# The last chunk's output stage of an attention + FFN layer, split into two halves of 256 tokens

## The reference, cut to what matters

```python
h = _layernorm(x) * (1 + ca) + sa
x = x + ga * _L0_attn_ref(h, Wq, Wp, bp)        # 16 heads of 16, softmax over all 4096 tokens
h = _layernorm(x) * (1 + cb) + sb
x = x + gb * _L0_ffn_ref(h, ...)
# _L0_ffn_ref: residual + 0.5 * (silu(layernorm(h)*gamma+beta @ w1 + b1) @ w2 + b2), hidden width 1024
```

## Time and profile before

| | |
|---|---|
| time, median of 3 runs | 2159.39 us (2160.18, 2159.39, 2154.71) |
| time of the profiled execution | 2153.64 us |
| its span, first to last instruction | 2151.0 us |
| busy in the span | PE 91%, ACT 92%, DVE 18%, POOL 4% |
| mean granted TensorE clock | 0.986 of full speed |
| last two exponentials of the attention start | 2083.94 us |

### The profile page before, as it was taken

How to read it: one execution, slowest core, us unless ns; L and a number is a source line. 1 busy time by engine, 2 the same in 40 slices (tenths; PEclk the granted TensorE clock), 3 DMA queues, 4 the chain that set the end, 5 groups by cost and what they waited for, 6 DMA issues and landing times.

```text
span 2151.0 us, 32823 instructions
## 1 busy us (share of the span) xinstructions
PE 1965.8 (91%) x13703; PEld 537.4 (25%) x13703; DVE 392.8 (18%) x873; ACT 1979.6 (92%) x2161; POOL 91.7 (4%) x42
## 2 busy tenths in 40 slices
PE   5578889999999999999999999999999999999995
PEld 3411112222222222222222222222222222222233
DVE  7501000410022100411004100311004100221003
ACT  2489999999999999999999999999999999999971
POOL 2000000100000000100001000100001000010001
PEclk9889999999999999999999999999999999999998
DMA  3261111111211111212121121212121112111100
GB/s 129 80 180 48 48 40 48 44 43 40 53 46 47 49 49 44 51 32 58 39 55 43 44 53 39 49 46 51 40 57 41 47 39 54 44 39 39 29 11 10
DMA packets 121860, 107.38 MB, mean 50 GB/s; under 512 B 23025, under 2 KB 120945, under 8 KB 121457
## 3 DMA queue, kind: packets, MB, share of 16 engines
q1 hardware_dynamic: 121712, 105.29, 18.0%
HBM read 96.56 MB, written 8.65 MB: 49 GB/s over the span
## 4 chain that ended last, share of the span: by engine, by line
ACT 48%; PE 39%; issue 7%; DVE 1%; DMA 0%; SPq 0%; ACTq 0%
ACT attend_probs L686 47%; PE attend_sums L724 18%; PE attend_scores L712 10%; PE attend_out L756 5%; PE attend_out L751 2%; PE attend_out L742 1%; ACT attend_half_tanh L671 1%; PE attend_scores L751 1%; PE attend_scores L756 1%; PE attend_out L747 0%; PE attend_scores L742 0%; DVE attend_rsqrt_work L92 0%; DVE attend_st L874 0%; DVE attend_rs L87 0%; PE attend_scores L747 0%
## 5 line engine op out<-in xcount | busy, mean ns | idle before, releaser
L686 ACT ACTIVATE attend_probs<-attend_scores 128x1024 f32<-128x1024 f32 x2048 | 1909.1, 1046 | 39.7 <-PE attend_scores L712 23.6
L724 PE MATMUL attend_sums<-attend_probs,values 128*17 128x512 f32 x8192 | 1010.8, 597 | 0.0
L712 PE MATMUL attend_scores<-asks,keys 64*128 64x512 f16 x4096 | 658.2, 383 | 109.5 <-ACT attend_probs L686 69.2
L712 PEld LDWEIGHTS attend_scores<-asks,keys 64*128 64x128 f16 x4096 | 149.5, 94 | 883.3 <-ACT attend_probs L686 778.0
L724 PEld LDWEIGHTS attend_sums<-attend_probs,values 128*17 128x17 f32 x8192 | 171.7, 96 | 394.8 <-issue 390.4
L756 PE MATMUL attend_out<-w,hidden 128*128 128x256 f32 x448 | 125.9, 403 | 0.0
L751 PE MATMUL attend_out<-attend_ffn_in,w 128*128 128x512 f32 x224 | 124.6, 638 | 0.0
L846 DVE COPY attend_sums_sb<-attend_sums 128x512 f32<-128x512 f32 x32 | 22.1, 691 | 499.2 <-PE attend_sums L724 499.2
L910 DVE TENSOR_SCALAR attend_half_in<-attend_out,b_col 128x512 f32<-128x512 f32 x56 | 42.0, 750 | 351.1 <-PE attend_out L751 350.1
L756 PEld LDWEIGHTS attend_out<-w,hidden 128*128 128x128 f32 x448 | 75.9, 189 | 95.1 <-issue 89.3
L920 DVE TENSOR_TENSOR attend_base<-attend_out,attend_base 128x512 f32<-128x512 f32 x14 | 9.7, 691 | 393.2 <-PE attend_out L756 393.2
(11 more groups left out here) (129 smaller groups left out, 568.7 us busy)
## 6 DMA issues: line engine op xcount, KB each, us to landing
keys<-parts_dram SPq DMA_DIRECT2D x768, 64.0 KB
keys<-parts_dram SPq DMA_DIRECT2D x256, 56.0 KB
asks<-parts_dram SPq DMA_DIRECT2D x192, 64.0 KB
start_x_in<-L_attn_x SPq DMA_DIRECT2D x8, 512.0 KB, 6.5
parts_dram<-start_q_parts SPq DMA_DIRECT2D x16, 256.0 KB, 2.5
attend_x_now<-L_attn_x SPq DMA_DIRECT2D x8, 512.0 KB, 4.2
out<-attend_base SPq DMA_DIRECT2D x16, 256.0 KB, 2.7
asks<-parts_dram SPq DMA_DIRECT2D x64, 56.0 KB
```

The costliest lines, as they stand in the source:

```text
L686: act.activation(probs[n % P_RING], ps_scores[:, 2 * slot:2 * slot + 2, :], ACT.Exp, scale=scale)\
L712: last = pe.matmul(ps_scores[:, 2 * (n % S_RING) + b, :], keys[rows, part % K_RING, hq, col:col + P], asks[rows, group * Q_HEADS + hq, :], ...
L724: last = pe.matmul(ps_sums[32 * hq:32 * hq + E1, :], values[:, j + STEPS * b, (gg % Q_GROUPS) * Q_HEADS + hq, :], probs[n % P_RING][:, b, ...
```

## The change

The tail works on two halves of 256 tokens (two tiles each). DVE does the whole chain residual, norm, modulation, norm for half 0 and then for half 1. PE transposes, does up and down for half 0, then the same for half 1; the up matmuls have 256 columns instead of 512. The evacuation of the transposed `z2` goes from DVE to ACT (Identity with scale and bias, L697 of the changed kernel). SiLU has 256 columns, 16 instructions instead of 8. `base` of the last chunk is computed by DVE, per half, behind both norm chains; POOL does it for the other seven chunks as before. The second half's projection and down result are in `ps_out`. New semaphores order this. Code of the other chunks is unchanged.

```diff
@@ GpSimd
                     pool.tensor_tensor(x_now, x_now, wide(bp_ga[:, :]), ALU.add).then_inc(xb_ready, 1)
+                    if o == G - 1:
+                        break
@@ ScalarE
-                o = G - 1
-                for f in range(FT):
-                    act.wait_ge(up_mm, FT * o + f + 1)
-                    act.activation(hidden[:, f, :], ps_scores[:, f % 4, :], ACT.Silu, bias=b1_col[:, f:f + 1]).then_inc(tail_hidden, 1)
+                for half in range(2):
+                    cols = slice(half * D, (half + 1) * D)
+                    act.wait_ge(tail_turned, half + 1)
+                    for k in range(DC):
+                        act.activation(ffn_in[:, k, cols], ps_scores[:, 4, k * D:(k + 1) * D], ACT.Identity,
+                                       bias=beta_col[:, k:k + 1], scale=gamma_col[:, k:k + 1]).then_inc(tail_in, 1)
+                    for f in range(FT):
+                        act.wait_ge(tail_up, FT * half + f + 1)
+                        act.activation(hidden[:, f, cols], ps_scores[:, f % 4, 0:D], ACT.Silu, bias=b1_col[:, f:f + 1]).then_inc(tail_hidden, 1)
@@ TensorE
-                pe.wait_ge(z2_ready, o + 1)
-                for k in range(DC):
-                    turn_z2(k, ps_scores[:, 4 + k, :])
-                pe.wait_ge(fi_ready, 2 * o + 2)
...
+                for half in range(2):
+                    cols = slice(half * D, (half + 1) * D)
+                    pe.wait_ge(z2_ready, o + half + 1)
+                    wait(pe, tail_in, DC * half)
+                    for k in range(DC):
+                        for t in range(2):
+                            last = pe.transpose(ps_scores[:, 4, k * D + t * P:k * D + (t + 1) * P],
+                                                z2[:, 2 * half + t, k * P:(k + 1) * P], ident[:, :])
+                    last.then_inc(tail_turned, 1)
+                    pe.wait_ge(tail_in, DC * (half + 1))
                     for f in range(FT):
+                        wait(pe, tail_hidden, FT * half + f - 3)
+                        for k in range(DC):
+                            last = pe.matmul(ps_scores[:, f % 4, 0:D], w1[:, k, f * P:(f + 1) * P], ffn_in[:, k, cols],
+                                             start=(k == 0), stop=(k == DC - 1))
+                        last.then_inc(tail_up, 1)
+                    for t in range(2):
+                        for f in range(FT):
+                            if t == 0:
+                                pe.wait_ge(tail_hidden, FT * half + f + 1)
+                            last = pe.matmul([ps_scores[:, 5, :], ps_out][half][:, t * D:(t + 1) * D],
+                                             hidden[:, f, (2 * half + t) * P:(2 * half + t + 1) * P], w2[:, f, :],
+                                             start=(f == 0), stop=(f == FT - 1))
+                    last.then_inc(tail_down, 1)
@@ VectorE
+                for half in range(2):
+                    pair = slice(2 * half, 2 * half + 2)
+                    residual(o, half, [ps_scores[:, 2, :], ps_out][half])
+                    dve.wait_ge(x1_ready, 2 * o + half + 1)
+                    stats_of_half(x1, half, 0)
+                    scaled_half(z1, x1, half, 0).then_inc(z1_ready, 1)
...
+                    dve.tensor_tensor(hid[:, pair, :], z1[:, pair, :], wide2(mod[:, 4, :]), ALU.mult).then_inc(scaled, 1)
...
+                    dve.tensor_tensor(hid[:, pair, :], hid[:, pair, :], wide2(mod[:, 3, :]), ALU.add).then_inc(hid_ready, 1)
...
+                    stats_of_half(hid, half, 1)
+                    scaled_half(z2, hid, half, 1).then_inc(z2_ready, 1)
+                dve.wait_ge(y_stored, 32 * o)
+                for half in range(2):
...
+                    dve.tensor_tensor(base[:, pair, :], hid[:, pair, :], wide2(mod[:, 5, :]), ALU.mult).then_inc(tail_base, 1)
...
+                    dve.tensor_tensor(base[:, pair, :], base[:, pair, :], wide2(b2_gb[:, :]), ALU.add).then_inc(tail_base, 1)
...
+                    dve.tensor_tensor(base[:, pair, :], base[:, pair, :], x1[:, pair, :], ALU.add).then_inc(tail_base, 1)
...
+                    dve.wait_ge(tail_down, half + 1)
+                    dve.tensor_tensor(base[:, pair, :], [ps_scores[:, 5, :], ps_out][half].rearrange("p (t d) -> p t d", d=D),
+                                      base[:, pair, :], ALU.add).then_inc(y_ready, 1)
```

More of the change, by code:

```diff
@@ L584, in adaln_layer @@
          base_step, z2_ready, z2_turned, fi_ready, up_mm, half_ready, tanh_done, hidden_ready, down_mm, y_ready, y_stored,
-         tail_hidden) = (sem(n) for n in (
+         tail_turned, tail_in, tail_up, tail_hidden, tail_down, tail_base) = (sem(n) for n in (
              "xn_in", "xb_ready", "att_turned", "af_ready", "proj_mm", "x1_ready", "n_stats", "n_mom", "n_rstd", "z1_ready",
              "scaled", "hid_ready", "base_step", "z2_ready", "z2_turned", "fi_ready", "up_mm", "half_ready", "tanh_done",
-             "hidden_ready", "down_mm", "y_ready", "y_stored", "tail_hidden"))
+             "hidden_ready", "down_mm", "y_ready", "y_stored", "tail_turned", "tail_in", "tail_up", "tail_hidden", "tail_down", "tail_base"))
         z2 = z1
@@ L825, in _ @@
                         pe.wait_ge(af_ready, 2 * o + 2)
-                    project(t, ps_scores[:, 2 + t // 2, (t % 2) * D:(t % 2 + 1) * D])
-                pe.wait_ge(z2_ready, o + 1)
-                for k in range(DC):
-                    turn_z2(k, ps_scores[:, 4 + k, :])
-                pe.wait_ge(fi_ready, 2 * o + 2)
-                for f in range(FT):
-                    if f >= 4:
-                        pe.wait_ge(tail_hidden, f - 3)
-                    for k in range(DC):
-                        up(f, k, ps_scores[:, f % 4, :])
@@ L836, in _ @@
-                for t in range(GT):
-                    for f in range(FT):
-                        if t == 0:
-                            pe.wait_ge(tail_hidden, f + 1)
-                        down(t, f, ps_scores[:, 4 + t // 2, (t % 2) * D:(t % 2 + 1) * D])
+                    project(t, [ps_scores[:, 2, :], ps_out][t // 2][:, (t % 2) * D:(t % 2 + 1) * D])
+                for half in range(2):
+                    cols = slice(half * D, (half + 1) * D)
+                    pe.wait_ge(z2_ready, o + half + 1)
+                    wait(pe, tail_in, DC * half)
+                    for k in range(DC):
+                        for t in range(2):
[3 more added lines that the diff above has]
+                    pe.wait_ge(tail_in, DC * (half + 1))
+                    for f in range(FT):
+                        wait(pe, tail_hidden, FT * half + f - 3)
[11 more added lines that the diff above has]
+                    last.then_inc(tail_down, 1)
@@ L995, in _, with wide2 @@
                     take_att(o, k, ps_scores[:, k, :])
[L996 to L1003, removed]
+                def wide2(v):
+                    return v.unsqueeze(1).broadcast_to([P, 2, D])
@@ new lines, in stats_of_half @@
+                def stats_of_half(src, half, r):
+                    n = 2 * o + 2 * half + r
+                    tiles = range(2 * half, 2 * half + 2)
+                    for t in tiles:
+                        last = dve.bn_stats(st2[:, t, :], src[:, t, :])
+                    last.then_inc(n_stats, 1)
+                    dve.wait_ge(n_stats, n + 1)
+                    for t in tiles:
+                        last = dve.bn_aggr(mo2[:, r, t, :], st2[:, t, :])
+                    last.then_inc(n_mom, 1)
+                    dve.wait_ge(n_mom, n + 1)
+                    pair = slice(2 * half, 2 * half + 2)
+                    rsqrt(dve, rs2[:, r, pair], mo2[:, r, pair, 1], rsqrt_work2[:, :, pair], n_rstd, n)
@@ new lines, in scaled_half @@
+                def scaled_half(to, src, half, r):
+                    for t in range(2 * half, 2 * half + 2):
+                        last = dve.tensor_scalar(to[:, t, :], src[:, t, :], mo2[:, r, t, 0:1], rs2[:, r, t:t + 1], ALU.subtract, ALU.mult)
+                    return last
+                dve.wait_ge(z2_turned, 2 * o)
+                dve.wait_ge(base_step, 3 * o)
+                for half in range(2):
+                    pair = slice(2 * half, 2 * half + 2)
+                    residual(o, half, [ps_scores[:, 2, :], ps_out][half])
+                    dve.wait_ge(x1_ready, 2 * o + half + 1)
+                    stats_of_half(x1, half, 0)
+                    scaled_half(z1, x1, half, 0).then_inc(z1_ready, 1)
+                    dve.wait_ge(z1_ready, o + half + 1)
+                    dve.tensor_tensor(hid[:, pair, :], z1[:, pair, :], wide2(mod[:, 4, :]), ALU.mult).then_inc(scaled, 1)
+                    dve.wait_ge(scaled, o + half + 1)
+                    dve.tensor_tensor(hid[:, pair, :], hid[:, pair, :], wide2(mod[:, 3, :]), ALU.add).then_inc(hid_ready, 1)
+                    dve.wait_ge(hid_ready, o + half + 1)
+                    stats_of_half(hid, half, 1)
```

(13 more changed lines are left out.)

## The result

The changed kernel takes 2146.94 us (median of 7 runs, 2144.39 to 2151.23). The kernel before took 2154.84 us (median of 7 runs, 2153.84 to 2160.18, the three of the forecast among them). The ratio is 0.9957, 95% interval 0.9942 to 0.9971: 0.43% faster, against 0.42% forecast. In absolute terms the forecast of 2150.4 lies 3.5 us too high, because it stood on the median of three runs of before, 2159.39; seven runs put that at 2154.84. The saving was forecast at 9.0 us; the two medians differ by 7.9, and the ratio makes it 9.3, with an interval of 6.2 to 12.5.

A forecast was written before the change was run, and what follows sets the result against it. The tail was taken as one serial chain, DVE then PE. Half 0's z2 10.16 us earlier, 0.62 less to up, 1.80 lost in matmuls: 8.98 saved, 2159.39 to 2150.4 us (0.42% less), range 2144.5 to 2156.

The forecast's parts named there:

- main case: Whole change: 7.5 to 9.5 us saved, 2149.9 to 2151.9 us on the median of before; chance 0.6.
- VectorE's chain: DVE's work for half 0 from residual to z2 takes 10.57 us, with 2.38 us of rsqrt in each norm.
- The evacuation pair: ACT's two evacuations of a half's transposed z2 take 1.04 us, with bounds of 0.78 and 1.56.
- The cold stretch: PE's clock stays at 1.2 GHz for the first 3.94 us of half 0's up, costing 1.97 us.
- A warm half: Up and down of one half on PE at full clock take 6.98 + 6.92 = 13.90 us.
- Base at nothing: Base on DVE behind both norm chains costs nothing, as PE covers it; uncovered, 2.2 us a half.
- The account of the 10.16 us: Half 0's z2 is ready for PE 10.16 us earlier: POOL stalls 4.0, second residual 1.7, smaller half 4.4.
- A second cold stretch: Rival: PE's clock falls again between the halves (2152.1 us), or its first low spell lasts longer (2152.4 us); chance 0.14.
- Only the stalls: Rival: the split gives back its gain and only the 4.0 us of POOL stalls stays, 2155.4 us; chance 0.12.
- The gain is bigger: Rival: the clock rises sooner or evacuations overlap better, 9.5 to 10.5 us saved, 2148.9 to 2149.9 us; chance 0.1.
- The cold clock holds on: Rival: PE's clock doesn't rise until the end of the tail, 17.3 us slower, 2176.7 us; chance 0.04.
- the rule: Skill's warning on thin matmul slices with waits: each half would begin at 1.2 GHz; a fall between halves costs 1.7 us.

The follow-up runs named there:

- experiment 6: Changed kernel with both evacuations of the transposed z2 on VectorE instead of ScalarE; ratio 0.9959 to the kernel before.
- experiment 4: Changed kernel plus ten additional matmuls (result never read) on TensorE ahead of half 0's transposes; ratio 0.9950 to the kernel before.
- experiment 1: Kernel before, tail unsplit, with only base of the last chunk moved from GpSimd to VectorE; ratio 0.9983 to the kernel before.
- experiment 2: Changed kernel, but base of the last chunk stays on GpSimd, all 1024 columns once both halves of hid are ready; ratio 0.9962 to the kernel before.
- experiment 3: Changed kernel, but GpSimd computes base of the last chunk per half, as soon as each half of hid is ready; ratio 0.9961 to the kernel before.
- experiment 7: Changed kernel with half 1's four transposes moved ahead of half 0's second down tile; ratio 0.9956 to the kernel before.
- experiment 10: Changed kernel once more, unaltered, for one profile; 52.69 us from the last copy of the sums to the last add.
- experiment 5: Kernel before, unsplit, with base of the last chunk on VectorE and fifteen additional matmuls ahead of the transposes; ratio 0.9977 to the kernel before.
- experiment 8: Changed kernel with half 1's transposes ahead of half 0's second down tile and ten additional matmuls ahead of half 0's transposes; 2141.05 us, ratio 0.9932 to the kernel before.

## Why the prediction was right

The sign, the size and the mechanism held: DVE's chain for half 1 lies under PE's work on half 0. That 0.42% met 0.43% to a hundredth is luck, since the interval of the ratio runs from 0.29 to 0.58%, and the two pairs of profiles give 8.25 and 6.95 us, both below the forecast's 8.98. The median of 2146.94 lies in the range, but below the 2149.9 to 2151.9 of the forecast's main case, since the median of before moved by 4.6 us. Term by term, with the forecast's saving of 8.98 us against 8.25 in the first pair:

| step | forecast us | measured us |
|---|---|---|
| arrival at the first residual, against before | 0 | +0.17 |
| VectorE's chain for half 0 | 10.57 | 10.62 |
| transposes to up, half 0 | 2.25 | 2.23 |
| up and down of half 0 | 15.87 | 16.22 |
| between the halves | 1.79 | 1.71 |
| up and down of half 1 to the last add | 13.93 | 14.19 |
| sum (the kernel before: 53.39) | 44.41 | 45.14 |

- **VectorE's chain** was right to 0.05 us, with `rsqrt` at its fixed cost. Each half pays it twice.
- **The evacuation pair** was put at 1.04 from bounds of 0.78 and 1.56, and took 1.02. That it is on ScalarE doesn't matter (experiment 6), so this part of the change is neutral.
- **The cold stretch** was taken as before, 3.94 us of up; it was 4.7, which is 0.4 us. The clock also fell earlier, at 2099.2 and not at 2101. The forecast had named a clock of 0.50 behind 2112 as a sign of being wrong; it was there until 2112.9, in a tail that began 0.8 us later, and changed no path. Experiment 4 removed the cold stretch and got 2.76 us back, transposes included.
- **A warm half** was put at 13.90; in experiment 4 half 0 takes 2121.65 - 2107.74 = 13.91. Half 1 takes 14.19, since it is counted to the last add, which starts some 0.28 us later than PE could have gone on; half 0's add too starts 0.27 us behind the transposes that follow its down matmuls (2124.65 against 2124.38). The forecast had 0.03 for this. Nor did up in pieces of 256 columns cost nothing: from the first up matmul to the first down matmul experiment 4 takes 7.01 us a half, 14.02 for both, and the kernel before 15.78 less 1.97 for the cold stretch, 13.81. That is 0.2 us.
- **Base at nothing** held; half 0's was done at 2118.4, 6 us ahead of its use, half 1's at 2127.4, 13 us ahead.
- **The account of the 10.16 us** was nearly right as arithmetic: in the count the first transposes start 9.94 us earlier, and of this the stalls are 4.4 by experiment 1, not 4.0. The forecast left out the third stall, L83 at 0.55 instead of 0.17 us. It was not right as cause: in a split tail GpSimd could have kept base, if it began when both halves were ready (experiment 2). The parts are substitutes and don't add.
- **A second cold stretch** didn't come in the wait between the halves, in any of the five profiles that have this wait and no additional matmuls. The forecast gave it 0.14. A fall behind short waits was real elsewhere. What the forecast said against it, that the full clock had outlasted the projection by 5 us and the short waits ahead of it, was a reading of one execution: in the changed kernel the clock fell 2.4 us behind the projection, and in experiments 3, 7 and 10 in the projection itself, after waits of 0.8 to 0.95 us.
- **Only the stalls** is refuted: base alone gives 0.9983, the change 0.9957, with intervals that don't meet, and experiment 2 has the gain with the stalls in place.
- **The gain is bigger** isn't shown: the ratio's 9.3 us is no more than its interval, and both pairs of counts are under 9.
- **The cold clock holds on** never came near: the rise came at most 6.0 us into up (experiment 3).

The Trainium skill (TensorE: Matmul & The Clock Gate, "HAM oscillation — how this bites in real kernels") describes slices of matmuls with waits between them, each of which starts at the low clock again. The trace agrees in one place: in experiment 5 the clock fell behind waits of 1.73 and 1.19 us, which cost 1.7 us. It does not agree between the halves, where the forecast had applied the rule: half 1 began at the full clock in all six profiles that have this wait, of 1.7 to 1.9 us with the transposes in it.

Open is why the clock fell in the projection in experiments 3, 7 and 10. Up to the projection's end the additional matmuls of experiments 4, 5 and 8 play no part, so it fell in three of eight profiles of split kernels and in none of four of whole ones, too few to tell chance from cause. The three are also the ones whose tail began latest of all thirteen profiles (2091.56 to 2093.15, the others up to 2091.44); by which way that could matter, no run shows. One kernel is left untried that would tell more: the change with matmuls only ahead of the projection.

## What to carry to other kernels

A serial tail in which one engine works and the next waits can gain from two pieces, if the fixed steps of a piece (here 2 x 2.38 us of `rsqrt`) are smaller than the work of the other engine that they are laid under. Cost it as a path from one row to the next, and look at what PE does between the pieces: here moving four transposes took that wait away (1.36 us in experiment 7). When two parts of a change remove the same wait, one of them may be all of it: try each alone. Measure a tail from an event at its start, not by the span.

## What was unexpected of the hardware

The place where the granted clock falls and rises isn't fixed by the program alone: in two executions of the changed kernel it fell 2.4 us behind the projection and inside it, and rose 4.7 and 4.1 us into up. Over all kernels with a cold start of up the rise came 3.9 to 6.0 us into it. Where the fall came behind the projection, it came 2.1 us (experiment 2) to 5.4 us (the kernel before) after its end. In experiment 10 PE had stood still for no more than 0.94 us at a time, three times, before it fell in the projection. A low spell in the projection, or at the start of up in experiment 5, cost 1.3 to 1.7 us, as much as one of the smaller edits was worth, so an edit of that size needs a profile of each piece rather than a time. VectorE's evacuation of 128x256 from PSUM takes 0.99 us for two, no faster than ScalarE's 1.02.
